# Two tensors kept in device memory in a linear-attention and mixture-of-experts kernel: the transposed input for the query stage, and the residual of the second half

## The reference

```python
# first half: linear attention with 16 heads of 16, 64 features a head
q, k, v = heads(x @ Wq + bq), heads(x @ Wk + bk), heads(x @ Wv + bv)
qp, kp = relu(q @ rw) + 1e-6, relu(k @ rw) + 1e-6
kv     = einsum('bhsf,bhsd->bhfd', kp, v)                # summed over the 2048 rows
out    = (qp @ kv) / (qp @ kp.sum(rows) + 1e-6)
x1     = layernorm(x + out @ Wo + bo)
# second half: a gated MLP plus 1024 single-row experts chosen by two-part keys
mlp    = silu(x1 @ Wg + bg) * (x1 @ Wu + bu) @ Wd + bd
w      = silu(x1 . down_embed[idx]) * softmax(top-8 scores)   # 4 heads, 8 experts each
y      = layernorm(x1 + mlp + sum(w * up_embed[idx]))
```

## Time and profile before

| | us |
|---|---|
| median of 3 runs | 3693.36 (3690.94 to 3703.25) |
| the profiled execution, its own time | 3696.48 |
| its span, first to last instruction | 3694.6 |
| PE busy | 3556.8 (96%) |
| VectorE busy | 2884.5 (78%) |
| ScalarE busy | 1907.5 (52%) |
| GpSimd busy | 1483.7 (40%) |
| granted TensorE clock, mean | 0.991 |

### The profile page before, as it was taken

One profiled execution on the slowest core, in us unless ns is written; L12 is line 12 of the kernel. 1 busy time (PEld: TensorE's weight loads), 2 busy tenths in 40 slices (PEclk: granted clock), 3 DMA queues, 4 the chain that ended last, 5 costly groups with the idle time before them and its releaser, 6 DMA issues.

```text
span 3694.6 us, 52250 instructions
## 1 busy us (share of the span) xinstructions
PE 3556.8 (96%) x19420; PEld 2927.6 (79%) x19420; DVE 2884.5 (78%) x5810; ACT 1907.5 (52%) x2502; POOL 1483.7 (40%) x1012
## 2 busy tenths in 40 slices
PE   8779999999999999999999999999999999999988
PEld 6568888888888888888788888788888888877767
DVE  4588778888778887788887777887778887888883
ACT  4455455555455555455555455555555554555541
POOL 0344344443344433344443344434444433444430
PEclk9889999999999999999999999999999999999999
DMA  3000000000000000000000000000000000000000
GB/s 116 18 12 18 10 15 12 18 18 12 12 18 12 18 18 12 12 18 12 18 18 12 12 18 12 18 18 12 13 14 16 18 12 7 12 12 12 7 6 12
DMA packets 23339, 61.17 MB, mean 17 GB/s; under 512 B 5552, under 2 KB 10032, under 8 KB 23088
## 3 DMA queue, kind: packets, MB, share of 16 engines
q1 hardware_dynamic: 18480, 41.04, 3.5%
q0 software_dynamic: 4608, 16.78, 1.1%
HBM read 41.04 MB, written 16.78 MB: 16 GB/s over the span
## 4 chain that ended last, share of the span: by engine, by line
PE 74%; DVE 13%; ACT 7%; issue 3%; POOL 2%; SPq 0%; DMA 0%; DVEq 0%; ACTq 0%; POOLq 0%
PE ring L639 22%; PE y_bank L732 10%; PE y_bank L734 9%; PE step_bank L562 5%; PE step_bank L666 5%; PE step_bank L639 4%; PE step_bank L598 3%; PE step_bank L590 3%; PE step_bank L656 3%; PE step_bank L548 3%; PE step_bank L712 2%; PE step_bank L554 2%; ACT grid L866 2%; DVE narrow L1097 2%; POOL grid L461 2%
## 5 line engine op out<-in xcount | busy, mean ns | idle before, releaser
L461 POOL TENSOR_TENSOR grid<-ex 128x1024 f32<-128x1024 f32 x512 | 1049.0, 2056 | 858.5 <-ACT prob L870 322.7
L732 PE MATMUL y_bank<-wd_sb,gate 128*128 128x256 f32 x2048 | 622.6, 386 | 2.4 <-DVE wexp L1139 2.4
L734 PE MATMUL y_bank<-up_sb,wexp 128*128 128x256 f32 x2048 | 609.7, 379 | 0.0
L1104 DVE SCALAR_TENSOR_TENSOR grid<-grid,best 128x1024 f32<-128x1024 f32 x256 | 328.2, 1282 | 250.9 <-POOL grid L461 246.6
L1117 DVE SCALAR_TENSOR_TENSOR prob<-grid,narrow,prob 128x1024 f32<-128x1024 f32 x256 | 472.3, 1845 | 6.8
L639 PE MATMUL ring<-x1T_hl,downT_hl 128*128 128x512 f32 x1536 | 424.0, 411 | 17.6 <-ACT gate L876 17.6
L639 PE MATMUL ring<-x1T_hl,wg_hl 128*128 128x512 f32 x1536 | 427.3, 413 | 5.4 <-DVE gate L1133 5.4
L734 PEld LDWEIGHTS y_bank<-up_sb,wexp 128*128 128x128 f32 x2048 | 389.6, 190 | 52.6
L448 POOL TENSOR_SCALAR qp<-qp 128x512 f32<-128x512 f32 x256 | 249.5, 974 | 437.5 <-ACT qp L850 427.0
L639 PE MATMUL ring<-x1T_hl,wu_hl 128*128 128x512 f32 x1536 | 421.1, 409 | 0.0
L876 ACT ACTIVATE gate<-ring,bg_sb 128x512 f32<-128x512 f32 x256 | 176.0, 687 | 440.6 <-PE ring L639 439.5
(11 more groups left out here) (159 smaller groups left out, 6115.4 us busy)
## 6 DMA issues: line engine op xcount, KB each, us to landing
xb<-in_L_attn_x SPq DMA_DIRECT2D x34, 512.0 KB, 3.7
out_y<-x POOLq DMA_DIRECT2D x32, 512.0 KB, 3.0
xa<-in_L_attn_x SPq DMA_DIRECT2D x30, 512.0 KB, 3.7
prob<-in_L_ffn_down_embed SPq DMA_DIRECT2D x1, 1024.0 KB, 5.6
prob<-in_L_ffn_Wg SPq DMA_DIRECT2D x1, 1024.0 KB, 8.4
prob<-in_L_ffn_Wu SPq DMA_DIRECT2D x1, 1024.0 KB, 10.6
wd_sb<-in_L_ffn_Wd SPq DMA_DIRECT2D x1, 1024.0 KB, 11.6
up_sb<-in_L_ffn_up_embed SPq DMA_DIRECT2D x1, 1024.0 KB, 12.5
```

The source lines that it names most:

```text
L461: pool.tensor_tensor(grid[:, h % 2], bcast(ex[:, h, 0:NX].unsqueeze(2), [P, NX, NK]), bcast(ex[:, RH + h, 0:NK].unsqueeze(1), [P, NX, NK]) ...
L732: pe.matmul(rows, gate[:, c % 2, t * P:(t + 1) * P], wd_sb[:, c, :], start=(c == 0 and t % 2 == 0), stop=False, skip_group_check=True)
L734: mm = pe.matmul(rows, wexp[:, c % 2, t * P:(t + 1) * P], up_sb[:, c, :], start=False, stop=(c == C - 1), skip_group_check=True)
L1104: marks["keep", h] = rt_steps.mark(dve.scalar_tensor_tensor(out=g, in0=g, scalar=best[:, h, TOP - 1:TOP], in1=g, op0=ALU.is_ge, op1=ALU.mult))
```

## The change

Two tensors in device memory are new. `xT_kept` takes the transposed x of each group when the key stage has made it; four rounds later a DMA brings it back as `xbT`, and the attention stage's two `turn` uses are gone from `AT_SEQ` (the other uses keep their chunks and gaps). `x1_kept` takes x1 when its layernorm is done; a DMA brings it back into `x1` (also `y_sb`) once the `next` transposes have read it and the copy is stored. POOL adds `bd` to it (a new instruction in chunk 0, after the first `spread`), and VectorE's `y_rows` adds it to the sums. PE's 16 products at line 728 are gone. `y_rows` moves from the head of chunk 0 to chunk 1 behind `ff_h(1)`, `norm2` from chunk 0 to the end of chunk 1, POOL's inverse root for it to chunk 1, and the output DMA to the head of chunk 2. POOL's addition of `bo` no longer waits for the query stage's `turn`.

```diff
-    AT_SEQ = ([("turn", 0), ("turn", 1), ("q", 0), ("q", 1)] + ...
+    AT_SEQ = ([("q", 0), ("q", 1)] + ...
+    xT_kept = nc.dram_tensor("xT_kept", [NG, P, KD, G], F32).ap()
+    x1_kept = nc.dram_tensor("x1_kept", [NG, P, T, D], F32).ap()
...
+            def keep(a):
+                lane, i = in_lane(a)
+                sp.wait_ge(*drained("kv", a, "turn", 0))
+                sp.wait_ge(*drained("kv", a, "turn", 1))
+                sp.dma_start(xT_kept[a], lane.xT[:]).then_inc(lane.kept, 16)
...
                 if at:
                     if m == 0:
-                        sp.wait_ge(*full("kv", 2 * FILL - 1, "turn", 1))
+                        sp.wait_ge(*full("kv", 2 * FILL - 1, "sum", T - 1))
+                        sp.wait_ge(xbT_kept, FILL * 16)
                     else:
+                        sp.wait_ge(*full("at", m - 1, "wo", 1))
+                    lane, i = in_lane(m)
+                    sp.wait_ge(lane.kept, (i + 1) * 16)
+                    sp.dma_start(xbT, xT_kept[m]).then_inc(xbT_loaded, 16)
+                    if m:
                         sp.wait_ge(*drained("at", m - 1, "wo", 1))
                     sp.dma_start(xb[:], x_groups[m]).then_inc(xb_loaded, 16)
+                if 0 < m <= NG:
+                    sp.wait_ge(x1_ready, m * T)
+                    sp.dma_start(x1_kept[m - 1], x1[:]).then_inc(x1_stored, 16)
+                if last:
+                    sp.wait_ge(*full("at", min(m, NG) - 1, "next", 1))
+                    sp.wait_ge(x1_stored, min(m, NG) * 16)
+                    wait(sp, y_stored, f * 16)
+                    sp.dma_start(x1[:], x1_kept[f]).then_inc(res_loaded, 16)
+                if kv:
+                    keep(a)
...
# POOL
                     pool.wait_ge(xb_loaded, (m + 1) * 16)
-                    pool.wait_ge(*full("at", m, "turn", 1))
                     pool.tensor_tensor(xb[:], xb[:], bcast(bo_sb ...
...
+                    if last and c == 2:
+                        pool.wait_ge(y_ready, (f + 1) * T)
+                        pool.dma_start(out_groups[f], y_sb[:]).then_inc(y_stored, 16)
...
-                    if last and c == 0:
-                        norm_scale(y_dve, (f + 1) * Y_STEPS, ln2_pool, f, mv2, rstd2, rstd2_ready)
...
+                    if last and c == 1:
+                        norm_scale(y_dve, (f + 1) * Y_STEPS, ln2_pool, f, mv2, rstd2, rstd2_ready)
...
-                    if last and c == 1:
-                        pool.wait_ge(y_ready, (f + 1) * T)
-                        pool.dma_start(out_groups[f], y_sb[:]).then_inc(y_stored, 16)
+                    if last and c == 0:
+                        pool.wait_ge(res_loaded, (f + 1) * 16)
+                        pool.tensor_tensor(x1[:], x1[:], bcast(bd_sb[:].unsqueeze(1), [P, T, D]),
+                                           ALU.add).then_inc(res_ready, 1)
...
# PE
-                        if c == C - 2:
-                            for k in range(KD):
-                                for part in range(2):
-                                    pe.matmul(rows[:, k * P:(k + 1) * P],
-                                              x1T_hl[:, par, part, k, t * P:(t + 1) * P], ident_r[:],
-                                              start=False, stop=False, skip_group_check=True)
...
# ScalarE, first turn of a key group
+                        act.wait_ge(lane.kept, i * 16)
...
-                    if kind == "turn":
-                        read_by(act.copy(xbT[:, j, :], at_bank[:]), "at", m, kind, j)
...
# VectorE, y_rows
-                    if m:
-                        dve.wait_ge(*full("at", min(m, NG) - 1, "next", 1))
-                    wait(dve, y_stored, f * 16)
+                    dve.wait_ge(res_ready, f + 1)
                     for i in range(2):
                         dve.tensor_tensor(y_sb[:, 2 * i:2 * i + 2, :], pair(y_bank[i]),
-                                          bcast(bd_sb[:].unsqueeze(1), [P, 2, D]), ALU.add).then_inc(y_read, 1)
+                                          y_sb[:, 2 * i:2 * i + 2, :], ALU.add).then_inc(y_read, 1)
```

More of the change, by code:

```diff
@@ L1179, in body @@
                         ff_h(c)
+                    if last and c == 1:
+                        y_rows()
                     if rt and not odd:
@@ L1203, in body @@
                         add_head(t, 3), clamp(t)
+                    if last and c == 1:
+                        norm2()
                 assert not rt or rt_steps.k == RT_STEPS
```

47 lines of the change are left out of this document (24 added, 23 removed).

## The result

The changed kernel takes 3736.21 us (median of 4 runs, 3733.87 to 3736.88); the kernel before took 3694.76 in the runs beside it (median of 4, 3690.94 to 3703.25). The ratio is 1.0108, with a 95% interval of 1.0089 to 1.0126: about 40 us slower. The runs of the kernel before lie in two groups, near 3695 and near 3706 us, with mean granted clocks near 0.991 and 0.987; its profile is of the first, and there is none of the second. The prediction had 3707, with a range from 3648 to 3755. The direction is right; 29 us are missing, and 3736 is outside the narrower range that it gave for its own mechanism (3690 to 3728). The profiled execution took 3735.98, its span is 3734.2, and the mean granted clock is 0.975 where it was 0.991.

A forecast was written before the change was run, and what follows sets the result against it. PE was taken as the bound, busy 109.19 of 110.90 us a round. Saved work and new waits netted +11.6 + 8 - 3 - 4 + 1 = +14, giving 3707 us; 8-in-10 range 3648 to 3755, own range 3690 to 3728.

The forecast's parts named there:

- What comes off PE: Two turns (1.05 us) and four residual products (1.92) leave PE: 3.0 us a round and group, 95 over 32 groups.
- The copies: SP's four new 512 KB DMAs a round stay hidden, cost zero; 3.7 us a round if the cover were gone.
- The start of a round: POOL's earlier `bo` addition holds VectorE's `keep`, delaying PE's routing product in chunk 0: 1.5 us of 3.0 lead lost.
- Chunk 1: PE's `ff_out(0, 0)` waits for `y_rows`: 3.6, 1.65, 3.1 us in rounds like 21, 19, 20; net 1.9, 1.1, 3.1.
- Behind it: After chunk 1 VectorE is 3.5 to 4 us later, but line 975's bank has 2.1 us margin: counted zero.
- the slower rival: Line 975 too late, PE waits at line 666, 1.5 to 2 us in each of 29 rounds: 3757; chance 0.14.
- The sum: Whole kernel: +11.6 + 8 - 3 - 4 + 1 = +14 us, giving 3710 profiled, 3707 as median.
- Only the second wait: Early `bo` addition delays nothing PE needs at round start; only the chunk 1 wait remains: 3664; chance 0.15.
- only the first: Round-start wait stands; `y_rows` in chunk 1 is late by only 1.4 us in all rounds: about 3665; chance 0.12.
- the full gain: Neither the round-start nor the chunk 1 wait holds PE: 3693 - 95 + 1 = 3600; chance 0.05.

The follow-up runs named there:

- 11: Kernel before, nothing kept in device memory; only `y_rows` additions placed late in chunk 0, statistics, normalisation and store in chunks 1 and 2: 3706.67 us.
- 9: Changed kernel with POOL's `bd` addition first in its round and `y_rows`' two additions moved to chunk 0, statistics staying in chunk 1: 3651.95 us, ratio 0.9877.
- experiment 3: Changed kernel with POOL's addition of `bd` moved to the head of its round, ahead of `bo`; `y_rows` stays in chunk 1: 3704.81 us.
- Experiment 6: Changed kernel with POOL's addition of `bo` waiting until the routing product of chunk 0 is done: 3707.45 us.
- 1: Kernel before with only `y_rows`, `norm2`, the inverse root and the store moved as in the change; nothing kept in device memory: 3751.14 us.
- experiment 2: Changed kernel with PE repeating `ff_weights(1)` transposes to fill its wait for `y_rows`: 3723.53 us, ratio 1.0051.
- 4: Changed kernel with PE's second k projection of chunk 1 ahead of the first output sum: 3738.99 us.
- 5: Changed kernel with `y_rows`, normalisation and store back in chunk 0 behind the exponentials, and `bd` first on POOL: 3714.02 us.
- 7: Only the transposed x kept in device memory; residual on PE and y banks read in chunk 0 as in the kernel before: 3726.94 us.
- experiment 10: Changed kernel with POOL's `bd` addition first and PE's wait for the y banks filled with repeated transposes: 3691.47 us, ratio 0.9972.

## Why the prediction was right, and where it was off

**What comes off PE: over-sized.** From 11 to 9, the same placement, PE is busy 82.5 us less, where the prediction had 95. A turn was worth 0.42 us instead of 0.52, and the residual 1.73 a group instead of 1.92: the distances between two starts that the prediction read held more than the products' own cost.

**The copies: right.** They cost PE nothing that a run shows; where an engine did wait for one (POOL, 2.23 us in experiment 3), nothing of PE hung on it.

**The start of a round: right in mechanism, half the size.** `keep` is held to 2.82 us, as assumed; PE waits 0.80, not 1.5. Line 952 ends at 2034.43 in it, PE would have been there 0.80 earlier: the lead of PE that the wait eats is smaller than 3.0, and `keep` ended later by 1.55 instead of 1.8. Experiment 6 shows the hold as the cause.

**Chunk 1: right in mechanism and size.** The forecast was 3.6, 1.65 and 3.1 us; measured are 3.23, 1.49, and in rounds like 20 1.5 to 2.3 behind 1.91 for `blocks`. The time at which `y_rows` should run, from the frame of round 21, was 12.6 to 13.9 us into the round, and it ran from 12.3 to 13.6. The old wait of 1.71 is swallowed, as said. Rounds 33 to 35 wait 3.5 us there and 2.2 at the routing product, where 2 or so each was the net forecast.

**Behind it: right for the changed kernel**, where `qkv` does not wait. Other orders show how near it was: 0.48 us there in some rounds of experiments 1 and 2, 1.01 in 4, up to 1.49 in rounds like 20 of 9. The time of 3736 lies between the forecast (3707) and the slower rival (3757), but that rival's wait is not what made it.

**The sum.** In the prediction -95 of work and +109 of waits, net of the old ones, gave +14. In the profiles it is -82.5 of work, +72.0 of idle time, and a third term that the prediction did not have: the remaining products take 50.1 us longer (3524.4 - 3556.8 + 82.5). The three give +39.6, the difference of the spans, as they must: the third is what busy time is left when the work, measured in other kernels, is taken out. The third term fits the granted clock: span times one less clock is 33 us before and 93 after, 60 more, part of it in idle time. The forecast's two terms were both too large, the work by 12.5 us and the waits by 37, and the excess of waits stood in for most of the 50 us that it left out. That 3707 came as near as 29 us is therefore in part luck. The step that was off is that a wait was priced at its length alone. The kernel before had 1.71 us of waiting in each such round with the clock at 1.00 throughout, and I took that for a property of the kernel instead of one of the wait. The Trainium skill, "TensorE: Matmul & The Clock Gate", section "HAM oscillation — how this bites in real kernels", says that where a long enough gap comes back in every turn of a loop, the engine starts slow in every turn. The trace agrees for the rounds like 21 and 20, all of which lose clock; in those like 19 a wait of 1.49 us left it at 1.00. Where only some turns with the same wait lose clock (experiments 1, 3, 5 and 7), the measurement goes beyond what that section says.

**The rivals.** "Only the second wait" is refuted by experiment 6, where taking away the hold by `bo` gains 28.8 us; "only the first" by the 3.23 us in front of line 756, where it had 1.4 in all rounds; the full gain of 3600 is not reached even by the ninth experiment, whose old waits remain.

**What stays open.** Which rounds of the same kind lose clock with the same wait (experiments 1, 3, 5 and 7), or with no wait (the start of rounds like 20), is not explained by any row of the timeline; I did not try to control it.

## What to carry to other kernels

When work is taken off the engine that bounds, ask first where it will now wait, and ask of each recurring wait on TensorE two prices: its length, and what the next products take at the lower clock (here 1.7 us a time behind 3.23 us, 3.4 in rounds like 20, and nothing behind 1.49 in rounds like 19). Work moved to make room should go into a hole of the receiving engine: moving the same two additions from chunk 1 into such a hole was worth some 50 us (experiments 3 and 9). And where VectorE and GpSimd both do elementwise work in SBUF, an instruction that is moved on one of them can be an added wait on the other.

## What the runs showed of the hardware

- TensorE at the lower clock: after idle times of 3.23 us in every round, after 1.90 in every full round like 20 of the changed kernel, where a second wait follows, after 2.73 and 2.28 in some rounds and not in others, not after 1.71, 1.63 or 1.49 in the full rounds like 21 and 19 shown here, and after 1.01 where products of 34 columns follow. In some rounds also with no idle time, behind sixteen products of 33 columns. A fall cost 1.7 us, in some rounds twice that, with pairs of 256 columns at 0.86 us instead of 0.43.
- Adding 644 (experiment 2) or 584 (experiment 10) useless products in front of a wait made the kernel 13 us faster, both times.
- VectorE and GpSimd hold each other: 2.82 against 1.27 us for `keep`, 2.17 for an instruction on two numbers a partition, 3.38 against 2.36 for the addition of `bo`, and 3.03 against 1.38 for `norm2`, whose one large input and output are in SBUF.
